# Gathering per-sample tables by row with indirect DMAs into SBUF, in place of copies in DRAM

## The reference, cut to what matters

```python
x = x + einsum('bct,bcd->bdt', x, W0[cond])                # 16 tables of 64x64
x = x + lora_ffn(x, lora_key)                              # F = 2752, rank 16, 16 adapters
x = x + s4d(x, length)                                     # causal convolution of 1024 times, mask
x = x + einsum('bct,bcd->bdt', x, W3[subj]) + bias3[subj]  # 32 tables of 64x64

def lora_add(base, inp, A, B):                             # for gate, up and down
    t = einsum('bri,bni->bnr', A[key], inp)
    return base + einsum('bor,bnr->bno', B[key], t) * 0.5

gate, up = lora_add(x @ Wg.T, x, Ag, Bg), lora_add(x @ Wu.T, x, Au, Bu)
down = lora_add((silu(gate) * up) @ Wd.T, silu(gate) * up, Ad, Bd)
```

## Time and profile before

| what | value |
|---|---|
| median of 3 runs | 1816.24 us (1814.32 to 1817.92) |
| the profiled execution, its own time | 1816.11 us |
| its span, first to last instruction | 1814.5 us |
| mean granted TensorE clock | 0.978 of full speed |
| PE busy / DVE / ACT / POOL | 1715.8 / 1129.6 / 687.0 / 175.2 us |
| DMA: packets, bytes, mean rate | 106660, 269.52 MB, 149 GB/s |
| of it the queue of POOL | 12544 packets, 36.29 MB |

### The profile page before, as it was taken

The page is one execution under the profiler, slowest core; times in us unless marked ns, Lnnn a source line. Parts: engine busy times, 40 slices in busy tenths (PEclk is TensorE's granted clock), DMA queues, the critical chain, the costliest instruction groups (busy, mean ns, idle before and its releaser), DMA issues.

```text
span 1814.5 us, 29058 instructions
## 1 busy us (share of the span) xinstructions
PE 1715.8 (95%) x8904; PEld 1470.7 (81%) x8904; DVE 1129.6 (62%) x1695; ACT 687.0 (38%) x1095; POOL 175.2 (10%) x282
## 2 busy tenths in 40 slices
PE   5679999999998999998999999999989899999998
PEld 5568888888888888886888888888877778879997
DVE  2566676676665554334666766766657843448887
ACT  3233333333333443232333333333323422236655
POOL 3442000000000000000000000000010004402330
PEclk9789999999999999999999999999989999999999
DMA  5787233233325564554333333332325534467754
GB/s 196 216 272 212 94 112 102 92 107 103 99 87 197 174 214 162 206 175 147 111 102 99 103 105 98 107 104 90 101 80 182 177 133 140 162 240 238 240 178 186
DMA packets 106660, 269.52 MB, mean 149 GB/s; under 512 B 17142, under 2 KB 22038, under 8 KB 105590
## 3 DMA queue, kind: packets, MB, share of 16 engines
q1 hardware_dynamic: 81334, 210.54, 35.6%
q0 software_dynamic: 12544, 36.29, 6.2%
q10 hardware_dynamic: 12736, 22.16, 3.2%
HBM read 225.12 MB, written 61.64 MB: 158 GB/s over the span
## 4 chain that ended last, share of the span: by engine, by line
PE 44%; DVE 5%; issue 1%; SPq 1%; ACT 1%; DMA 0%; ACTq 0%; DVEq 0%
PE ps L1070 30%; PE ps L1320 5%; PE ps L1317 3%; PE ps L1108 2%; PE ps L1349 1%; DVE whl L1721 1%; PE ps L1333 1%; SPq L435 1%; PE ps L1145 1%; PE ps L1147 1%; DVE act_hl L1725 0%; DVE x1s L1735 0%; SPq L432 0%; DMA wraw<-in_wd 0%; ACT whl L744 0%
## 5 line engine op out<-in xcount | busy, mean ns | idle before, releaser
L1070 PE MATMUL ps<-act_hl,whl 128*128 128x512 f32 x2016 | 466.0, 393 | 10.6 <-DVE act_hl L1725 7.1
L1070 PE MATMUL ps<-xop,aop_a 128*128 128x512 f32 x2016 | 474.4, 391 | 0.0
L1070 PEld LDWEIGHTS ps<-act_hl,whl 128*128 128x128 f32 x2016 | 379.8, 189 | 95.1 <-DVE act_hl L1725 11.5
L1070 PEld LDWEIGHTS ps<-xop,aop_a 128*128 128x128 f32 x2016 | 374.1, 189 | 74.5
L1070 PE MATMUL ps<-xop,aop_b 128*128 128x512 f32 x1512 | 367.7, 392 | 6.8 <-DVE t L1687 6.7
L1070 PEld LDWEIGHTS ps<-xop,aop_b 128*128 128x128 f32 x1512 | 280.1, 189 | 61.9 <-DVE t L1687 6.9
L1721 DVE TENSOR_TENSOR whl<-wraw,whl 128x1024 fp32r<-128x1024 f32 x96 | 118.9, 1238 | 244.7 <-ACT whl L744 244.2
L744 ACT ACTIVATE whl<-wraw 128x1024 fp32r<-128x1024 f32 (+2 forms) x132 | 114.9, 887 | 357.9 <-PE ps L1070 289.1
L1658 DVE TENSOR_TENSOR aop_b<-raw,aop_b 128x512 fp32r<-128x512 f32 x84 | 58.0, 691 | 107.7 <-ACT aop_b L744 107.6
L744 ACT ACTIVATE aop_a<-asum 128x512 fp32r<-128x512 f32 x84 | 48.7, 625 | 163.9 <-DVE asum L1650 160.2
L1108 PEld LDWEIGHTS ps<-t_hl,lb_hl 128*128 128x128 f32 x672 | 97.2, 190 | 9.9
(11 more groups left out here) (222 smaller groups left out, 2020.3 us busy)
## 6 DMA issues: line engine op xcount, KB each, us to landing
wraw<-in_wd SPq DMA_DIRECT2D x88, 512.0 KB, 3.4
raw<-in_wgu SPq DMA_DIRECT2D x168, 256.0 KB, 3.1
rtoep<-k_dram SPq DMA_DIRECT2D x64, 512.0 KB, 4.6
lb_raw<-bgu_of_batches SPq DMA_DIRECT2D x84, 256.0 KB, 3.9
act_raw<-act_dram SPq DMA_DIRECT2D x84, 256.0 KB, 3.4
act_dram<-t ACTq DMA_DIRECT2D x42, 256.0 KB, 2.0
act_dram<-u ACTq DMA_DIRECT2D x42, 256.0 KB, 2.0
xn<-in_x SPq DMA_DIRECT2D x16, 512.0 KB, 6.5
```

The lines of the kernel that those rows point to most:

```text
L1070: ins = pe.matmul(bank, wt, r, start=start and k == 0 and n == 0, stop=stop and k == nk - 1 and n == 2, skip_group_check=True)
```

## The change

The host lays out three tables so that one table row is one row of an SBUF tile. Each first-layer table stands twice, once with 64 blank columns behind and once in front (`block_rows`), so that 128 gathered rows of 512 B make a block diagonal at once; the last mixing's table has its bias as a 129th column. `bgu` becomes rows of 1 KB, one per adapter, rank row and frame. A new input `keys` holds the keys of the samples, repeated for 128 partitions. DVE computes row numbers from it at the start (`row_w`, `row_r`, `row_b`), and POOL gathers with indirect DMAs of 128 rows straight into the tiles.

Away go: `bgu_of` and all its copies, `w0_dram` and `wbd_b`, SP's 16 loads of tables, ACT's 8, the clearing of `wbd_a` and `wbd3`, the 64 small DMAs of the last mixing, and SP's waits for copies. `lr_raw` is 4 gathers per pass and `lb_raw` 4 per frame, all issued by POOL; for each frame but the first POOL adds 1 to the row numbers. `wbd_a` is 8 gathers, `wbd1` 8 (in the last frame of pass 0, into the memory of form Q1), `wbd3` 16. The identity of `wbd_a` is added in four parts of two pairs; that of `wbd1` by DVE in the last frame. POOL's new order is: constants and mask, `wbd_a`, lr of pass 0, ad copies of pass 0, lb of frame 0 behind a wait for the x sums, ad copies of pass 1, lengths, lb of frames 1 to 20, `wbd1`, the residual with lr of pass 1 in between, lb of pass 1.

```diff
 # SP
-                    sp.wait_ge(ids_in, 48)
+                    sp.wait_ge(ids_in, 16)
...
-                    sp.wait_ge(consts, 2)
-                    for b in range(2 * CB):
-                        k = sp.value_load(ids[0:1, 0, 2 * CB + b:2 * CB + b + 1], min_val=0, max_val=NLORA - 1)
-                        rows = slice(64 * (b % 2), 64 * (b % 2) + 64)
-                        sp.dma_start(wbd_b[rows, b // 2, rows], w0[k]).then_inc(w0_in[4], 16)
...
-                    sp.wait_ge(bgu_first_in, 16 * 2 * CB)
-                else:
-                    sp.wait_ge(bgu_in, 16 * 2 * CB * 2)
-                    sp.wait_ge(down_lo, 2 * NF)
-                load_lr(p)
...
-                load_lb(p, 0)
...
-                    sp.wait_ge(bgu_in, 16 * 2 * CB)
...
-                sp.wait_ge(lb_lo, lb_before)
-                load_lb(p, f)
...
-                    sp.wait_ge(prod, n_f(0, NF - 1, PER_F) + 1)
+                    sp.wait_ge(prod, n_f(0, NF - 1, PER_F) + 2)
                     load_x(1, range(KH))
-                    sp.wait_ge(prod, n_f(0, NF - 1, PER_F) + 2)
+                    sp.wait_ge(prod, n_f(0, NF - 1, PER_F) + 3)
                     load_x(1, range(KH, NQ))
-                    sp.wait_ge(prod, n_f(0, NF - 1, PER_F) + 3)
-                    sp.wait_ge(w0_stored, 16)
-                    sp.dma_start(wbd1[:, :, :], w0_dram[:, :, :]).then_inc(w0_back, 16)
 # POOL
+            def rows_of(dst, table, index, landed):
+                pool.indirect_dma_start(out=dst, out_offset=None, in_=table,
+                                        in_offset=bass.IndirectOffsetOnAxis(ap=index, axis=0)
+                                        ).then_inc(landed, 16)
+            def load_lr(p):
+                for i in range(4):
+                    rows_of(lr_raw[:, 2 * i:2 * i + 2, :].rearrange("p a b -> p (a b)"), bgu[:, :],
+                            row_r[:, 4 * p + i:4 * p + i + 1], lr_in)
+            def load_lb(p, f):
+                if f > 0:
+                    mine = row_b[:, 4 * p:4 * p + 4]
+                    pool.wait_ge(lb_lo, n_f(p, f, 1))
+                    pool.tensor_scalar(mine, mine, 1.0, None, ALU.add).then_inc(row_next, 1)
+                    pool.wait_ge(row_next, p * (NF - 1) + f)
+                for i in range(4):
+                    rows_of(lb_raw[:, 2 * i:2 * i + 2, :].rearrange("p a b -> p (a b)"), bgu[:, :],
+                            row_b[:, 4 * p + i:4 * p + i + 1], lb_in)
...
+            pool.wait_ge(rows_step, 1)
+            for n in range(NQ):
+                rows_of(wbd_a[:, n, :], w0[:, :], row_w[:, n:n + 1], w0_in[n // 2])
+            pool.wait_ge(rows_step, 5)
+            load_lr(0)
+            pool.wait_ge(ids_in, 16)
...
+            gather_ads(0)
+            pool.wait_ge(x_sum, 4)
+            pool.wait_ge(x_lo, 4)
+            pool.wait_ge(x0_stored, 16 * 2)
+            load_lb(0, 0)
+            pool.wait_ge(ad_gathered, 16 * 2 * CB)
+            gather_ads(1)
             pool.dma_start(len_i[:, :], length.partition_broadcast(P)).then_inc(par_in, 16)
...
+            for f in range(1, NF):
+                load_lb(0, f)
+            pool.wait_ge(prod, n_f(0, NF - 1, PER_F) + 1)
+            for n in range(NQ):
+                rows_of(wbd1[:, n, :], w0[:, :], row_w[:, NQ + n:NQ + n + 1], w0_in[4])
...
             residual_in(0, 1, 4)
+            pool.wait_ge(down_lo, 2 * NF)
+            load_lr(1)
             pool.wait_ge(x1_done, 2 * KB)
             pool.dma_start(x1_dram[1], x0r[:, 1, :, :]).then_inc(x1_stored, 16)
+            pool.wait_ge(x1_stored, 16 * 2)
+            load_lb(1, 0)
+            for f in range(1, NF):
+                load_lb(1, f)
...
+            for n in range(PAIRS):
+                rows_of(wbd3[:, n, :], w3[:, :], row_w[:, PAIRS + n:PAIRS + n + 1], w3_in)
+            pool.wait_ge(w3_in, 16 * PAIRS)
 # DVE
+            ts(row_w[:, :], keys_i[:, 0:2 * PAIRS], float(P), part_f[:, 0:1], ALU.mult,
+               ALU.add).then_inc(rows_step, 1)
...
+            for i in range(NQ // 2):
+                dve.wait_ge(w0_in[i], 16 * 2)
+                add_identity(wbd_a[:, 2 * i:2 * i + 2, :], 2).then_inc(w0_ready, 1)
...
+                elif p == 0:
+                    dve.wait_ge(w0_in[4], 16 * NQ)
+                    add_identity(wbd1[:, :, :], NQ).then_inc(w0_ready, 1)
                 dve.wait_ge(prod, n + 7)
                 dve.wait_ge(ev, e + 2)
                 tt(t5[:, :], ps[:, BE, :], t5[:, :], ALU.add).then_inc(ev, 1)
...
-                if first:
-                    dve.wait_ge(w0_stored, 16)
                 sums(p, 0)
```

More of the change, by code:

```diff
@@ L45 @@
 REST_S = STEPS - 1
+KEYS = 2 * PAIRS + 2 * NCH
 LS = 32
@@ L57, with build @@
 TWO_PI = 6.283185
-def build(nc, x, cond, lora, length, subj, w0, wgu, wrest, wd, agu, ad, bgu, bd, log_dt, c_ri, log_ar, a_im,
-          d_skip, w3, bias, out):
+def build(nc, x, lora, keys, length, w0, wgu, wrest, wd, agu, ad, bgu, bd, log_dt, c_ri, log_ar, a_im,
+          d_skip, w3, out):
     ctx = ExitStack()
@@ L369, in load_unit @@
                     at = p * 2 * CB + u * HB + b
-                    k = sp.value_load(ids[0:1, 1, at:at + 1], min_val=0, max_val=NLORA - 1)
+                    k = sp.value_load(ids[0:1, at:at + 1], min_val=0, max_val=NLORA - 1)
                     sp.dma_start(dst[:, b, :], agu[k]).then_inc(w_in[buf], 16)
[L373 to L379, removed]
-                    sp.dma_start(lb_raw[rows, :, :], bgu_of[p, 1 + f].rearrange("q c h g m -> q (c h g) m")
-                                 ).then_inc(lb_in, 16)
             def load_ad(p, g):
@@ L637, in _ @@
-            add_identity(wbd_b, NQ).then_inc(w0b_ready, 1)
-            pool.wait_ge(w0b_ready, 1)
-            pool.dma_start(w0_dram[:, :, :], wbd_b[:, :, :]).then_inc(w0_stored, 16)
-            for c in range(2):
-                for half in range(2):
-                    with pool.Fori(0, HB) as b:
-                        gather_bgu(0, c, half, b, lora_key(0, c, half, b), 2, FB, bgu_in)
-            pool.dma_start(len_i[:, :], length.partition_broadcast(P)).then_inc(par_in, 16)
-            pool.wait_ge(ad_gathered, 16 * 2 * CB)
@@ L647, in _ @@
-            pool.wait_ge(bgu_in, 16 * 2 * CB)
-            for c in range(2):
-                for half in range(2):
-                    with pool.Fori(0, HB) as b:
-                        k = lora_key(1, c, half, b)
-                        gather_bgu(1, c, half, b, k, 0, FB, bgu_in)
-                        gather_ad(1, c, half, b, k)
+            pool.wait_ge(rows_step, 1)
+            for n in range(NQ):
+                rows_of(wbd_a[:, n, :], w0[:, :], row_w[:, n:n + 1], w0_in[n // 2])
@@ new lines, in _, with gather_ads @@
+            pool.wait_ge(rows_step, 5)
+            load_lr(0)
+            pool.wait_ge(ids_in, 16)
+            def gather_ads(p):
+                for c in range(2):
+                    for half in range(2):
+                        with pool.Fori(0, HB) as b:
+                            gather_ad(p, c, half, b, lora_key(p, c, half, b))
+            gather_ads(0)
[3 more added lines that the diff above has]
+            load_lb(0, 0)
@@ L1016, in pass_ @@
                 down_chunk(p, 1, {})
[L1018 to L1024 removed]
+            act.wait_ge(ids_in, 16)
+            act.activation(g0[0:1, 0:1], ids[0:1, 0:1].bitcast(F32), ACT.Silu).then_inc(silu_table, 1)
             act.wait_ge(silu_table, 1)
```

146 lines of the change are left out of this document (57 added, 89 removed).

## The result

The changed kernel took 1794.54 us, the median of 4 runs (1791.33 to 1797.23), where the kernel before took 1816.70 beside it (1814.32 to 1817.92): a ratio of 0.9874, with a 95% interval of 0.9853 to 0.9895. Forecast were 1797.0, 1784 to 1813, and faster with 0.84. The same kernel timed again beside the last experiments took 1791.14 (5 runs), a ratio of 0.9848 (0.9835 to 0.9862). The profiled execution after is the one of 1791.33, the fastest of its four, with a span of 1789.8 and a clock of 0.987; before it was 1814.5 and 0.978. So the two traces differ by 24.7 us of span, and the forecast of the sum was 19.1.

The account below looks back on a forecast made before the run. PE was taken to bound the middle frames, and late tables the first 131 us. 1816.1 - 4.9 - 10.2 - 0.7 - 4.0 - 9.5 + 10.5 + 1.2 - 1.5 = 1797.0 us, range 1784 to 1813.

Parts of the forecast that it names:

- Price of one indirect DMA: On POOL: 1.3 us from one gather of 128 rows to the next.
- a gather waits for DVE: Rival: each gather stands for DVE operations and costs 3.2 us, total 1829.4; gathers over 2.25 us had chance 0.16.
- Start: First layer: PE starts near 12.4 us and not 17.27, -4.9 us.
- the freed time is not taken: Rival, before frame 0: something else is late next, half of the first four terms (19.8) is lost, 1807 us; chance 0.16.
- lr_raw: First lora product of the rest: PE's wait of 10.70 us shrinks to about 1, -10.2 us with some clock.
- w0_stored: Second lora product of the rest: without DVE's 8.25 us wait, PE's 7.41 falls to 3.4, -4.0 us.
- frame 0: Frame 0 of pass 0: the 6.7 us wait and most of the slow clock go, -9.5 us.
- The queue of POOL: Frame 1: lb comes late behind pass 1's 16 ad gathers, PE stands 8.5 us, +10.5 with slow clock.
- S: Moment when x sums are done and SP issued frame 0's lb; frame 1's lb forecast at S + 45.9, allowed S + 37.4.
- End of pass 0: Last frame of pass 0: DVE's identity add delays the chain to the first A-down product, +1.2 us.
- pass 1: PE's 5.50 us wait for wrest in pass 1 shrinks as lr loads earlier, -1.5 us, between 0 and -4.
- Last mixing: Sixteen gathers replace 64 POOL issues under the last down chunk: no effect.

Follow-up runs that it names:

- lb_twice: Changed kernel with each frame's four lb gathers issued twice in a row, the second set once the first had landed; 1815.87 us.
- lr_first: Changed kernel with the four lr_raw gathers ahead of the eight of wbd_a; no total given, PE starts 6.26 us later, the units 1.82, frame 0 0.57.
- lr_last: Changed kernel with the four lr_raw gathers moved behind the 16 ad gathers of pass 0 in POOL's queue; 1809.51 us.
- ads_late: Changed kernel with pass 1's 16 ad gathers and the lengths moved behind the lb of frames 2 to 5; 1795.69 us.
- x_gated: Changed kernel with SP's second half of x held until PE had done two of the eight first-layer products; 1811.32 us.
- ads_early: Changed kernel with pass 1's 16 ad gathers right behind those of pass 0, with their own semaphore; no total given, frame 0 starts at 84.38 us.
- lr_mid: Changed kernel with the four lr_raw gathers behind the first four ad gathers of pass 0; 1798.35 us.
- act_order: Changed kernel with lr_mid's edit and unit 1's halves later in ACT's and DVE's order; 1791.28 us, ratio 0.9852 to the kernel before.
- best: Changed kernel with act_order's order, ads_late's edit and POOL's identity add of the last mixing later; 1784.83 us, ratio 0.9810 to the kernel before.

## Why the prediction was right, and where its steps were not

The verdict, the mechanism and the size were right, the sum partly by errors that cancel. The gain at the start was taken 3.2 us too large and the loss in frame 1 8.6 too large; a loss of 4.3 in pass 1 and a gain of 3.4 behind it were not forecast.

*Price of one indirect DMA.* 1.3 taken, 1.25 measured; beside working frames 1.02 + 0.30. Right. The lock of "a gather waits for DVE" (called the fourth rival, the third in the list) did not come: the longest lb gather took 1.44, and the rival needed 2.45. lb_twice shows it best: 8 gathers per frame, and the frames stay at 21.97.

*Start, mis-sized.* The step counted PE's earlier start in full, -4.9, as if the units came with it. PE started 5.48 earlier, but the units follow ACT's copies, and these stand behind unit 1's table and behind a hold of ACT. It measured 1.75; lr_first, 6.26 later at the start and 1.82 at the units, says the same. This is the rival "the freed time is not taken", for one of its four terms.

*lr_raw, w0_stored, frame 0.* -10.2, -4.0 and -9.5 against -10.23, -4.40 and -9.22: right in size, and lr_last gives 12.2 back. The size of w0_stored is partly luck: the wait of 7.41 fell to 4.28 and not to 3.4, and 1.3 of the 4.40 are unit 3's products, 12.74 where they took 14.00, at a granted clock of 1.00 where it was 0.90. Of unit 3's -1.31 the waits before units 2 and 3 gave only 0.2 (5.62 together, where they were 5.80); the rest went with the clock, 0.75 where it was 0.61. w0_stored and frame 0 were not undone by themselves; that they were the waits named is read from the traces (DVE now stands 3.80, for the raw block itself). For lr_raw the order was what counted, not the way the rows come: behind 16 ad gathers the same table costs as much as in the kernel before.

*The queue of POOL, mis-sized.* The mechanism is shown by ads_late, which takes the wait away, and by lb_twice, which makes it 9.50. The size failed in the sum up to S + 45.9: the 16 ad gathers took 25.3 us (79.17 to 104.45, with a stop of 4.47) and not the 30.5 of the earlier trace rows, and the row step and the four gathers with their landing 8.75 (ACT's split of lb started at 113.84) and not 9.6. So lb was there at S + 40.0, with S at 73.82: 2.6 late by the forecast's own bound of S + 37.4, of which 1.70 reached PE. The 2 us of slow clock behind the wait didn't come (1.00 in that stretch); they came in lb_twice, behind its wait of 9.50, where 12 products took 4.98 at a clock of 0.57 and take 2.91 in a steady frame.

*End of pass 0, pass 1.* +1.2 and -1.5 were forecast, -0.03 and -0.37 measured. The first was right in its mechanism, and the clock hides it. DVE's add stands in the chain as forecast, and PE waits for it (DVE, then PE):

```profile
542.30 1.22 DVE L1370 TENSOR_TENSOR wbd<-wbd,ident 128x1024 f32<-128x1024 f32 x1
```

```profile
547.69 2.05 PE L1052 MATMUL ps<-wbd,xn 128*128 128x128 f32 x16 [0.55 <-DVE u L1702]
```

The last 80 products of the first layer of pass 1 begin 34.18 us after the last frame's start, where it was 33.37: 0.81 later. They then take 10.42, where they took 11.26, at a granted clock of 0.85 where it was 0.78. In pass 1 the wait of 5.50 for wrest is 3.20, but the units keep only 1.06 of that, as the products ahead of the wait took 7.47 and not 5.99, and the down chunks of pass 0 lost 0.69. Small, and not tested by itself.

*Last mixing, wrong.* "Nothing" overlooked that a shorter POOL queue moves what stands behind it. The earlier trace rows had the price in plain view, 4.74 us on a DVE operation beside a POOL subtraction that reads the same tile, wbd3; the forecast used them for the gathers alone, and not for the add that the gathers release. It cost PE a wait of 1.58. The Trainium skill, page "SBUF — State Buffer", section "Who interferes with whom", says that a DVE instruction with two SBUF inputs contends with a GpSimd instruction that reads SBUF, and that such contention is an exclusive lock: 4.70 in place of 0.68 agrees. The same section puts a plain two-input DVE operation on the shared read side only, and infers that the generation of DMA descriptors needs the write side; the gathers' 1.02 us beside busy DVE agree with that.

## What to carry to other kernels

Price a gather by its issue (here 1.25 us for 128 rows, 4 us from the last issue to the split), but decide where it goes by what stands ahead of it and behind it in its queue: one table behind 16 copies cost 12 us, the same table ahead of them next to nothing. When a queue gets shorter, look up every instruction behind it: a tensor operation on POOL that slides from a pause of DVE into its work takes DVE away for its whole length (here 4.70 us beside 4.45). And a start that is moved forward is worth only what the next engine in the chain can take. Before two stretches are compared, compare their granted clocks: several steps here agreed with the forecast, or hid a loss, by the clock alone.

## What the runs showed of the hardware that was not expected

With the four lr gathers issued from 14.5 to 19.2 us, ACT's first copy came at 18.5 to 21.5 in seven profiles (in an eighth, x_gated, its second), the releaser not named by the profile in most of them; with lr elsewhere, behind ads, it came at 15.75 to 15.90 in four of four. SP's table issues were drawn out too (4 issues in 10.39 us, where they took 4.00 in the kernel before). ACT's stands of 5.2 to 9.8 us in the last chunk, beside 16 gathers, look alike, but came in only nine of the thirteen profiles with these gathers. What is held, an instruction or a signal, no run here settles.

Where the 16 ad gathers are issued in one go, POOL stops once, near the last issue, for 3.2 to 8.4 us (4.47 in the row above at 103.57, 7.63 in ads_early, 8.36 in x_gated): its length is no constant to forecast with. Where lr's gathers stand among the 16 (lr_mid, act_order, best), no stop among them was longer than 1.8.
